# A state-space block and a table-weight feed-forward on one core: comparisons, decay steps, residuals and pair loads put elsewhere in the order of the two decode stages

## What is computed

```python
# block 1, state space
proj = u @ W_in.T                      # z 512, x 512, B 64, C 64, dt 8
xBC  = silu(causal depthwise conv of 4 taps over (x, B, C) + conv_b)
dt   = softplus(dt_toks + dt_bias); dA = exp(-dt * exp(A_log))
S    = S * dA_t + dt_t * B_t * x_t     # scan over the tokens, state 64 for each of 512
y    = (S . C_t + D_param * x) * silu(z);  out = y @ W_out.T
# block 2, feed-forward with weights from a table
gate, up = x @ lut[gate_idx].T, x @ lut[up_idx].T        # 1376 wide
out  = (silu(gate) * up) @ lut[down_idx].T
```

## Time and profile before

| what | value |
|---|---|
| median of 3 runs | 1389.15 us (1387.81 to 1389.20) |
| the profiled execution's own time | 1389.16 us |
| its span, first to last instruction | 1387.0 us |
| TensorE matmul busy | 1302.5 us, 94% |
| VectorE busy | 973.6 us, 70% |
| ScalarE busy | 544.9 us, 39% |
| GpSimd busy | 532.9 us, 38% |
| mean granted TensorE clock | 0.98 |
| L1535 comparisons, 320 | 119.5 us, mean 434 ns |
| L1258 decode matmuls, 640 | 127.7 us, mean 354 ns, 21.1 us idle before |
| L611 segments, 64 | 122.4 us, mean 1933 ns |

### The profile page before, as it was taken

One profiled execution on the slowest core, in us unless ns is written; L12 is line 12 of the kernel. 1 busy time (PEld: TensorE's weight loads), 2 busy tenths in 40 slices (PEclk: granted clock), 3 DMA queues, 4 the chain that ended last, 5 costly groups with the idle time before them and its releaser, 6 DMA issues. The chain is left out here.

```text
span 1387.0 us, 18643 instructions
## 1 busy us (share of the span) xinstructions
PE 1302.5 (94%) x6656; PEld 630.1 (45%) x6656; DVE 973.6 (70%) x1895; ACT 544.9 (39%) x986; POOL 532.9 (38%) x723
## 2 busy tenths in 40 slices
PE   4778898988999999999999999999999999999997
PEld 2334444534444444444444445444444444444443
DVE  7889998998578756875687668865886555544332
ACT  5556576756434234332334243423443223132120
POOL 1433354434434434435333534364345344400102
PEclk9899999989999999999999999999999999999999
DMA  5144234422321224013302330142213212401201
GB/s 170 38 108 104 71 105 107 123 67 78 84 54 31 69 75 87 23 52 107 84 24 61 99 92 23 35 126 61 54 31 88 51 45 45 108 31 31 77 0 53
DMA packets 132812, 96.16 MB, mean 69 GB/s; under 512 B 102000, under 2 KB 102000, under 8 KB 132720
## 3 DMA queue, kind: packets, MB, share of 16 engines
q1 hardware_dynamic: 130832, 94.94, 26.6%
q10 hardware_dynamic: 1888, 0.03, 0.1%
HBM read 54.05 MB, written 16.78 MB: 51 GB/s over the span
## 5 line engine op out<-in xcount | busy, mean ns | idle before, releaser
L1352 PE MATMUL bank<-fxt,ffn_hi 128*128 128x512 f16 (+1 forms) x1408 | 420.3, 380 | 9.1 <-DVE gact L1684 7.5
L1352 PE MATMUL bank<-fxt,ffn_lo 128*128 128x512 f16 (+1 forms) x704 | 267.4, 380 | 0.0
L1352 PEld LDWEIGHTS bank<-fxt,ffn_hi 128*128 128x128 f16 (+1 forms) x1408 | 139.9, 100 | 179.8 <-DVE gact L1684 10.5
L1258 PE MATMUL bank<-mask,diag 128*128 128x416 f16 x640 | 127.7, 354 | 21.1 <-ACT ffn_lo L873 11.4
L646 POOL TENSOR_TENSOR state<-state,ex 64x512 f32<-64x512 f32 x32 | 37.5, 1173 | 262.0 <-PE bank L1315 260.8
L1366 PE MATMUL bank<-ffn_hi,h_hi 128*128 128x512 f16 (+1 forms) x352 | 133.5, 379 | 0.0
L1366 PE MATMUL bank<-ffn_hi,h_lo 128*128 128x512 f16 (+1 forms) x352 | 133.3, 379 | 0.0
L1366 PE MATMUL bank<-ffn_lo,h_hi 128*128 128x512 f16 (+1 forms) x352 | 133.3, 379 | 0.0
L611 POOL TENSOR_TENSOR decay<-causal_h,da 128x1024 f16<-128x1024 f16 x64 | 122.4, 1933 | 22.1 <-PE bank L1319 17.1
L1535 DVE TENSOR_SCALAR mask<-codes_h 128x832 f16<-128x832 f16 x320 | 119.5, 434 | 5.0 <-PE bank L1258 4.6
L1684 DVE SCALAR_TENSOR_TENSOR gact<-gact,bank 128x512 f32<-128x512 f32 (+1 forms) x88 | 60.3, 685 | 86.2 <-ACT gact L912 85.4
(11 more groups left out here) (186 smaller groups left out, 2240.3 us busy)
## 6 DMA issues: line engine op xcount, KB each, us to landing
codes_sb<-codes SPq DMA_DIRECT2D x80, 208.0 KB, 3.5
ures<-u SPq DMA_DIRECT2D x32, 256.0 KB, 3.0
x_scratch<-x SPq DMA_DIRECT2D x32, 256.0 KB, 2.4
ut<-x_scratch SPq DMA_DIRECT2D x16, 512.0 KB, 4.4
xres<-x_scratch SPq DMA_DIRECT2D x32, 256.0 KB, 3.1
out<-dn SPq DMA_DIRECT2D x32, 256.0 KB, 2.0
ut<-u SPq DMA_DIRECT2D x15, 512.0 KB, 4.3
ffn_hi<-w_in_t SPq DMA_DIRECT2D x4, 580.0 KB, 8.6
```

Source lines behind the costliest of these rows:

```text
L1258: last = nc.tensor.matmul(p.bank[:, 0:COLS], diag[:, q].rearrange("p n m -> p (n m)"), mask[:, n, q, j * COLS:(j + 1) * COLS], start=(q == ...
L1352: last = nc.tensor.matmul(bank, wt[:, c0:c0 + w], fxt[:, :, half, k, :], start=(k == 0 and n == 0), stop=(k == KC - 1 and n == 2))
```

## The change

On VectorE, `y_sum` of decode stages takes a count of a half unit. Four of its comparisons stand behind the first step of the sum, four behind the state add. The `masks` call that stood ahead of each of these `y_sum` is gone (for chunk 0 it stood at the end of the stage before). `time_steps` move ahead of `conv_silu` of block 0 and of masks(k + 10). `out_weights_low` moves ahead of `ln_stats`, and in stage 1 the pair's splits and statistics move behind one more half unit each. On GpSimd the decode stages get their own function, in which `add_residual` stands behind `weights`, not ahead of it. On ScalarE `normalise(t, 1)`, `normalise(t, 2)` and the two `normalise_slice` stand behind one more `decoded`. On SyncE three `load_pair` stand ahead of a `transpose_pair` rather than behind it. In the full stages `y_split(t, 0)` stands behind the two `ln_split`. No instruction is added or taken away.

```diff
@@ SyncE, decode_stage @@
                     if t == 0:
+                        load_pair("u", t + 1, 1)
                         transpose_pair("u", t + 1, 0)
-                        load_pair("u", t + 1, 1)
...
-                    transpose_pair("u", t + 1, 1)
                     if t + 1 < LAG:
                         load_pair("u", t + 2, 0)
+                    transpose_pair("u", t + 1, 1)
...
                         transpose_pair("x", t - 1, 0)
+                        load_pair("u", t + 2, 0)
                         transpose_pair("x", t - 1, 1)
-                        load_pair("u", t + 2, 0)
@@ GpSimd, new decode_stage; chunk 0, the others alike @@
+                    decay_state(t, 0)
+                    segments(t, 1)
+                    if t >= 1:
+                        out_rstd(t - 1, 3)
+                    weights(t, 1)
+                    if t >= 1:
+                        add_residual(t - 1, 3)
+                    pair_rstd("u", t + 1, 1)
@@ ScalarE, decode_stage @@
+                    decoded(t, 2)
                     if t >= 1:
                         normalise_slice("u", t + 1, 1, 0)
                         normalise_slice("u", t + 1, 1, 1)
-                    decoded(t, 2)
...
-                    normalise(t, 1)
                     codes_to_half(k + 14)
                     small(t, 3)
                     decays(t, 3)
                     decoded(t, 11)
+                    normalise(t, 1)
...
-                    normalise(t, 2)
                     z_tanh(t + 1, 0)
                     codes_to_half(k + 19)
                     small(t + 1, 0)
                     decays(t + 1, 0)
                     decoded(t, 16)
+                    normalise(t, 2)
@@ VectorE, y_sum @@
+                    y_steps.inc(nc.vector.tensor_tensor(
...
+                    if count is not None:
+                        for q in range(GROUP):
+                            one_mask(count, q)
...
                     state_ready.inc(nc.vector.tensor_tensor(state[to, :], state[h, :], tok_bank[h, :], ALU.add))
+                    if count is not None:
+                        for q in range(GROUP, PAIRS):
+                            one_mask(count, q)
@@ VectorE, decode_stage @@
-                    y_sum(t, 0)
+                    y_sum(t, 0, k + 1)
...
+                    masks(k + 3)
+                    if t >= 1:
                         ln_stats("u", t + 1, 1)
                     decayed(t, 1)
-                    masks(k + 3)
                     masks(k + 4)
                     if t == 0:
+                        out_weights_low()
                         ln_stats("u", t + 1, 1)
-                        out_weights_low()
...
+                    time_steps(t + 1)
                     conv_silu(t + 1, 0)
                     masks(k + 10)
-                    time_steps(t + 1)
-                    masks(k + 11)
...
-                    y_sum(t, 2)
+                    y_sum(t, 2, k + 11)
@@ VectorE, stage @@
-                    y_split(t, 0)
                     if nxt:
                         ln_split("u", t + 1, 0, 0)
                         ln_split("u", t + 1, 0, 1)
+                    y_split(t, 0)
```

48 lines of the change are left out of this document (30 added, 18 removed).

## The result

The kernel after takes 1399.12 us, the median of four runs (1398.56 to 1401.86), against 1388.74 us before in the same session (1387.81 to 1389.2). The ratio is 1.0071, with a 95% interval of 1.0054 to 1.0087: slower by 0.7%. The prediction said 1387.6 us, and its range ended at 1395.0. It was wrong in sign, and the time lies 4.1 us above the range.

What follows compares the result with a forecast made beforehand. Bound: TensorE and VectorE handing work over in decode stages, the y_split-to-gate_silu chain in full stages. Gains 9.5 (decode) + 0.7 (stage 2) - 5.2 (waits) - 3.4 (clock) = 1.6 us, 1389.2 to 1387.6 us; range 1380.5 to 1395.0.

Steps and rivals of the forecast that it cites:

- The price of the sum's comparisons: Decode stages: state adds wait for four comparisons, not eight; y_gated and y_split come up to 2.4 us later.
- The residual behind the weights: GpSimd, decode stages: residual next needed for a store some 10 us later, so costed at nothing; otherwise 1 to 2 us.
- move no wait that TensorE has in the rows: Decode stages: residual behind the weights, steps behind one more decoded, and codes in other order, given no gain or loss.
- The 3.68 us for ScalarE's bank: Stage 1, chunk 0: bank held while ScalarE waited to normalise the pair; 1.3 us of the wait was to remain.
- The gains of the decode stages: Stages 0 and 1: 6.0 and 3.5 us gained, together 9.5 us (4 to 13).
- The low half: Stage 0, project_out(0, 0): 5.5 us gained, less 2.0 for the load ahead of the transpose and 1.0 for later statistics: 2.5.
- the further microsecond: Stage 0, project_dt: if the transpose's data waits for all the load's, about another microsecond off the 2.5 us gain.
- Stage 2: First pair's load no longer behind a transpose, 2.0 us, against later y_split, 1.3 us: the 3.04 us wait shrinks by 0.7.
- Full stages: Stages 3 to 6: later y_split lengthens TensorE's gate_silu waits, 5.2 us lost; clock falls in two of four, 3.4 us.
- The rival that had it fall in all four: Full stages: later y_split decides, waits pass 2.0 us, clock falls in each, 12.0 us lost; 1393.5 us, chance 0.24.
- The rivals: Whole kernel: full clock kept, 1384.2 us (0.33); later y_split decides, 1393.5 (0.24); comparisons cover nothing, 1391.1 (0.06); forecast itself 0.37.
- scan (2, 0) at 350 or later (comparisons blocked by GpSimd): Start of stage 2: sign that would show the forecast wrong; the scan, at 354.02 before, was expected near 344.5.

Runs made afterwards that it cites:

- m: The kernel before with only the comparisons put inside the sum (four between multiply and add, four behind the state add): 1397.4 us, ratio 1.0059.
- c: The kernel after with the residual ahead of the weights again and y_split ahead of the two ln_split in the full stages: 1384.2 us, ratio 0.9959.
- f: c with the comparisons taken out of the sum, ahead of it again: 1382.0 us, ratio 0.9950.
- b: The kernel after with y_split(t, 0) ahead of the two ln_split again in the full stages: 1388.3 us, ratio 0.9993.
- e: b with the comparisons taken out of the sum, the residual still behind the weights: 1382.2 us, ratio 0.9947.
- d: The kernel before with only GpSimd's residual moved behind the weights in the decode stages: 1387.8 us, ratio 0.9991.
- a: The kernel after with only the residual put back ahead of the weights in the decode stages: 1393.6 us, ratio 1.0025.
- i: f with stage 1's statistics and splits of the pair put back early: 1377.8 us, ratio 0.9912; measured again at 1377.0 us, ratio 0.9904.
- r: i with SyncE's two loads of stage 0 behind their transposes again, stage 1's load left ahead: 1373.5 us, ratio 0.9883.
- g: c with time_steps behind masks(k + 10) again: 1387.3 us, ratio 0.9981.
- l: The kernel before with only out_weights_low moved ahead of ln_stats in stage 0: 1385.0 us, ratio 0.9970.

## Why the prediction was wrong, point by point

*The price of the sum's comparisons* is the step that failed most. The prediction named the delay, "up to 2.4 us later", and it was 1.9 to 2.0. It costed the gain (state adds that no longer wait) at 3.7 us in chunk (0, 2) and 2.7 in (1, 3), and the loss at 0.7 us in (0, 3) and 2.4 in (1, 0), with no clock in it. In m, chunk by chunk, the step gains 0.1 in (0, 2) and loses 1.9 in (1, 3), 4.7 in (0, 3) and 2.7 in (1, 0) and (1, 1). It never worked out how late `y_split` may come: the cover in (0, 3) was 0.6 us. Alone the step costs 8 us (m), within the other steps 2 (c against f) to 6 (b against e).

*The residual behind the weights, costed at nothing.* The cover named was the store some 10 us later. No wait in the rows above is for the residual itself. What moved is the weights: they no longer stand behind GpSimd's wait for `normalise`, so they start when `y_split` is at its last steps, 2.5 us of contention that had been apart. In chunk (0, 3) this also needs ScalarE's new order, whose effect on the weights was not costed either (d against e). Alone the residual's move costs nothing (d), in the company of the comparisons 2 to 4 us by decode length, 4 to 5.5 by time (a and c against after and b).

*Stage 1's statistics* have no term in the prediction, unless they are among the steps that "move no wait that TensorE has in the rows". The 3.68 us for ScalarE's bank did not hang on them but on GpSimd's turn, and the prediction let 1.3 of them remain. In c and f 4.0 did, and undoing the late statistics gave 3.5 to 5 us, of which 0.45 us is their own delay and the rest clock. In after 1.62 did, close to the 1.3, because the residual stands behind: the number is right there by luck, as that reason was not costed.

*The gains of the decode stages.* Run i leaves out just these three steps (and the swap of the full stages), so it measures what was costed as gain. Its decode length is 7.7 to 7.9 us shorter than before, against 9.5 forecast. By chunk, forecast and measured: chunks (0, 0) and (0, 1) 2.5 and 3.8; (0, 2) 2.3 and 2.0; (0, 3) 1.2 and 0.2, since TensorE now waits 1.72 us for `z_gate` there; (1, 0) and (1, 1) 2.0 and 3.0; (1, 2) -1.2 and 0.2; (1, 3) 2.7 and -1.4. The last was credited to the comparisons in the sum, which i does not have; its loss is the second clock fall shown with run r. The agreement in (0, 2) is luck: the state add's 2.01 us were credited to the comparisons in the sum, yet they are gone in i, which has none there, and back (2.10 us) in g, which has them in the sum but time_steps behind. The list of long idle times had also left out two in chunk (0, 0), 2.34 and 2.15 us for comparisons, with the clock at half behind the second; no term hung on them.

*The low half.* 5.5 us for the wait and its clock were right, l gained 5.7 in that chunk. The 1.0 us for later statistics was wrong: they start at 91.37 us in l, not behind 91.88, since what they waited for was their load. The 2.0 us for the load ahead of the transpose was right, 1.8; the further microsecond held in the lower bound did not show.

*Stage 2.* Forecast 0.7, measured 2.2. In after the wait is 2.56 us, so 0.5 us of the gain is wait and 1.7 is clock, which did not fall behind it and which the forecast had left out. By the runs, the load ahead gave 3.8 (chunk (2, 0) falls from 39.5 to 35.7 us), as the whole 3.04 us wait sank to 0.91 and took 1.7 us of half clock with it; the later `y_split` took 1.65 back.

*Full stages.* Forecast 5.2 + 3.4 = 8.6 us lost, measured 8.9. The waits were to be 2.2 us and were 2.47, 2.35, 2.67 and 1.88; the clock was to fall in two of the four, and fell in stages 3 and 5. The rival that had it fall in all four was wrong on that. That two was the right count is in part luck: run a had one fall in the same four stages, and lost 6.6 us.

*The sum* in decode length: 7.8 gained by the good steps, then 3.5 lost by the statistics (nearly all clock), 3.3 to 5.2 by the comparisons and 1.8 to 3.6 by the residual, which gives the 2.8 us lost. This split holds for this order of steps only. In another one the residual takes 0.6 (f to e) and the comparisons 6.3 (e to b), so the three cost 10.5 us together, and no single share is the step's own. The rivals were all drawn as sizes of terms that the forecast had. None asked what would happen if a step taken at nothing were not nothing, and so the range was closed 4 us too low. The forecast itself named the sign: "scan (2, 0) at 350 or later (comparisons blocked by GpSimd)". It came at 357.10.

## What to carry to other kernels

When a step is moved on an engine, note when its successors end, counted from the event that starts the chunk, and when the other engine takes them; the difference is the cover (here 0.6 us), and every delay in the change is added up against this one number, also of steps that each cost nothing. An engine that stops waiting is a change of its own: ask what it will now run beside. And an idle time that may bring the clock down is priced with what the rows show of half clock behind such times, here 1.7 to 5.1 us on top of its own length, less the part of the half clock that lies in the idle time itself.
